# Twenty-four transfers of a convolution cycle, issued in six portions of four, one behind each phase of TensorE

## The chip, the cores and the metric

One core of one Trainium2 chip runs the whole kernel. The metric is the device time of the launch in microseconds (us). Engines are named PE (TensorE matmuls), PEld (its weight loads), DVE (VectorE), ACT (ScalarE), POOL (GpSimd) and SP (SyncE, which here only issues transfers). DMA is the transfer engines, sixteen of them for the core.

## The reference

The input is x, float32, 4 images of 16 channels and 512 x 512 pixels. Four layers follow one another. Layer 0 is a depthwise convolution, window attention and an MLP; layer 1 takes ten steps of a surface flow. Layers 2 and 3, of which the change touches the code, are a residual block each:

```python
def _L2_conv_ref(x, w1, b1, w2, b2):
    out = _conv2d_same(x, w1, b1)      # 3x3, 16 -> 16 channels, float32
    out = jax.nn.relu(out)
    out = _conv2d_same(out, w2, b2)
    return out + x
```

What enters layer 2 is 0.7 u + 0.3 x, where u is the result of the flow and x is the output of layer 0.

## The kernel before, in words

Three stages run one after another: attention_stage, surface_stage and conv_chain. The third, conv_chain, reads two scratch tensors in the chip's main memory, `flowed` (u) and `attended` (x of layer 1), and runs all four convolutions of layers 2 and 3 in one pass over the image, from top to bottom. What follows is about conv_chain alone.

The image's 512 rows are cut into 64 groups of 8 rows. Four groups are held of each input, in `us` and `xs`; `r` is the group's place among them, its number modulo 4. The partitions are 4 images by 32 (16 channels of even rows and 16 of odd rows).

Every engine runs the same sequence of cycles, t = -1 to 66 (`every_cycle`): a few written out, then a loop whose body holds four cycles (`Fori(4, LAST - 7, 4)`, so that it jumps back to its start 13 times), then a few written out again. In cycle t PE makes six phases, in this order:

- conv2 of group t, first half (96 matmuls; it signals c2_begun)
- conv3 of group t - 2 (192 matmuls; c3_made)
- conv2 of group t, second half (96; c2_made)
- conv4 of group t - 2, first half (96; c4_begun)
- conv1 of group t + 1 (192; c1_made)
- conv4 of group t - 2, second half (96; c4_made)

Each matmul is 32 x 32 weights over 512 columns, with a weight load of its own. conv1 and conv3 are written by `across` (L1292), conv2 and conv4 by `along` (L1306). ACT applies bias and ReLU behind conv1 and conv3 (`hide`, `deepen`). DVE mixes the inputs of group t + 2 (`mix`: a scaling of `xs`, then the sum into `image`), adds the residuals behind conv2 (`add_image`) and behind conv4 (`add_middle`, which fills `outs`, one of two buffers, and signals out_done).

SP issues 24 transfers a cycle of 128 KB each: 16 loads of group t + 4, in four quarters of four (quarters 0 and 1 from `flowed` into `us`, quarters 2 and 3 from `attended` into `xs`), and 8 stores of group t - 3. They are placed by `behind(made, m)`, a wait of SP until PE has signalled that phase of group m. Nothing else sets their order: SP's instructions run in the order in which they are written. At the edges of the image `behind` does nothing for a group that is not there. DVE's `mix` waits for all 16 loads of its group, `add_middle` for the stores from the buffer that it fills.

Of the kernel before, what the change touches and what calls it, by code (L numbers as in the profile page):

```python
# [1146 lines left out]
def conv_chain(nc, src, mix_with, dst, weights, bias, edge):  # L1147
# [3 lines left out]
    B, C, HP, W = src.shape  # L1151
# [3 lines left out]
    LAST = GROUPS  # L1155
# [3 lines left out]
    with ExitStack() as ctx:  # L1159
# [3 lines left out]
        def sem(n):  # L1163
            return ctx.enter_context(nc.semaphore("chain_" + n))
# [16 lines left out]
        taps_begun, paced = sem("taps_begun"), sem("paced")  # L1181
        c1_made, c2_begun, c2_made = sem("c1_made"), sem("c2_begun"), sem("c2_made")
        c3_made, c4_begun, c4_made = sem("c3_made"), sem("c4_begun"), sem("c4_made")
        hidden_done, middle_done, deep_done, out_done = (
            sem(n) for n in ("hidden_done", "middle_done", "deep_done", "out_done"))
        stored = [sem(f"stored{k}") for k in range(2)]

        def wait(eng, s, value):

            if not isinstance(value, int) or value > 0:  # L1190
                eng.wait_ge(s, value)

        def there(m):

            return not isinstance(m, int) or 0 <= m <= LAST
# [7 lines left out]
        def every_cycle(eng, cycle):  # L1203

            for t in range(-1, 4):
                cycle(t, t % 4)
            with eng.Fori(4, LAST - 7, 4) as t:
                for k in range(4):
                    cycle(t + k, k)
            for t in range(LAST - 4, LAST + 3):  # L1210
                cycle(t, t % 4)

        def outs_of(m):

            return range(1, G4) if first(m) else range(1) if final(m) else range(G4)
# [3 lines left out]
        @block.sync  # L1219
        def _(sp):  # L1220
            sp.dma_start(w_sb[:], weights).then_inc(w_in, 16)  # L1221
            sp.dma_start(b_sb[:, :], bias).then_inc(w_in, 16)  # L1222
            sp.dma_start(e_sb[:, :], edge).then_inc(w_in, 16)  # L1223

            def load(t, r, quarter):
                if isinstance(t, int) and not 0 <= t < GROUPS:
                    return
                if quarter == 0:
                    wait(sp, mix_done, t - 3)
                    sp.sem_inc(paced, 1)  # L1230
                to, of = ((us, src), (xs, mix_with))[quarter // 2]
                for b in range(B // 2 * (quarter % 2), B // 2 * (quarter % 2 + 1)):
                    for s in range(2):
                        rows = of[b, :, bass.ds(t * (2 * G4) + (PAD + s), 2 * G4 - 1), :]
                        sp.dma_start(to[Q * b + C * s:Q * b + C * s + C, r], rows[:, 0:2 * G4 - 1:2, :]).then_inc(loaded[r], 16)  # L1235

            def store(m, r):
                if not there(m):
                    return
                sp.wait_ge(out_done, m + 1)  # L1240
                sp.sem_inc(paced, 1)
                n, k = len(outs_of(m)), outs_of(m)[0]
                for b in range(B):
                    for s in range(2):
                        rows = dst[b, :, bass.ds(m * (2 * G4) + (2 * k - 2 + s), 2 * n - 1), :]
                        sp.dma_start(rows[:, 0:2 * n - 1:2, :],
                                     outs[Q * b + C * s:Q * b + C * s + C, r % 2, k:k + n]).then_inc(stored[r % 2], 16)

            def behind(made, m):

                if there(m):
                    sp.wait_ge(made, m + 1)
                    sp.sem_inc(paced, 1)

            def cycle(t, r):
                behind(c2_begun, t)
                load(t + 4, r, 0)
                behind(c3_made, t - 2)
                store(t - 3, (r - 3) % 4)
                behind(c2_made, t)  # L1260
                load(t + 4, r, 1)
                behind(c4_begun, t - 2)
                load(t + 4, r, 2)
                behind(c1_made, t + 1)
                load(t + 4, r, 3)

            for t in range(3):
                for quarter in range(4):
                    load(t, t, quarter)
                if t == 0:  # L1270
                    sp.wait_ge(loaded[0], 2 * LOADS)
            every_cycle(sp, cycle)
            store(LAST, LAST % 4)
            for k in range(2):
                sp.wait_ge(stored[k], LOADS * ((LAST - k) // 2 + 1))

# [237 lines left out]
```

## Time and profile before

| what | value |
| --- | --- |
| median of 3 runs | 26449.37 us |
| lowest and highest | 26434.21 and 26502.42 us |
| the profiled execution | 26468.22 us |
| its span, first to last instruction | 26466.4 us |
| mean granted TensorE clock | 0.988 |
| PE busy over the span | 25367.9 us, 96% |

The profile describes one execution, whose own time stands in the table; the rest of the times are of executions that were timed alone. "Idle before" an instruction is what its engine stood still; a releaser is what ended that, and "issue" means that the profile shows none. A share of DMA is the busy time of the sixteen engines over the stretch, averaged; the records of packets overlap a little, so that it can stand above 1. Times within a trace count from the span's start.

### The profile page before, as it was taken

The page shows a single profiled execution, that of the slowest core. Times are in us where ns is not written, and L with a number is a line of the kernel's source. Part 1 is how long each engine was busy: PE and PEld are TensorE (multiplying, and loading weights), DVE is VectorE, ACT ScalarE, POOL GpSimd, SP SyncE. Part 2 cuts the span into 40 slices and gives each one's busy share as a digit, 9 for nine tenths or more (in the row PEclk, how much of TensorE's full clock was granted, in tenths as well). Part 3 has the DMA queues.
Part 4 walks back from the last instruction along what each step waited for, and adds up shares of the span by engine and source line. Part 5 has one row for each costly group of instructions (what it writes and reads, how often), then busy time and mean ns, then how long its engine had stood idle before and what let it go on. Part 6 is the DMA issues. An engine that isn't in the chain of part 4 may idle for free. (4 is left out here: it accounts for less than half of the span.)

```text
span 26466.4 us, 783400 instructions
## 1 busy us (share of the span) xinstructions
PE 25367.9 (96%) x323352; PEld 12517.7 (47%) x323352; DVE 22786.0 (86%) x22077; ACT 22113.8 (84%) x19199; POOL 5851.4 (22%) x6804
## 2 busy tenths in 40 slices
PE   8999999899999999999999999999999999999799
PEld 5666666544444443443444444444534453444455
DVE  6666666699999999999999999999999999999222
ACT  6666666699989998999999899999999998999111
POOL 0000000023323332333233233323323332333000
PEclk9999999999999999999999999999999999999999
DMA  1111111188888888888888888888888888888665
GB/s 33 32 32 32 32 32 32 36 155 156 155 168 156 154 156 169 156 155 166 159 156 155 168 154 156 158 167 156 155 166 158 156 154 168 155 156 157 119 115 101
DMA packets 1550406, 3439.19 MB, mean 130 GB/s; under 512 B 547440, under 2 KB 679152, under 8 KB 1546480
## 3 DMA queue, kind: packets, MB, share of 16 engines
q0 software_dynamic: 805120, 2858.13, 59.7%
q1 hardware_dynamic: 742512, 536.63, 10.3%
q8 instruction: 2649, 43.40, 0.7%
q14 instruction: 125, 1.02, 0.0%
HBM read 294.21 MB, written 201.33 MB: 19 GB/s over the span
## 5 line engine op out<-in xcount | busy, mean ns | idle before, releaser
L910 PE MATMUL surf_ps<-surf_u,surf_matf 64*64 64x512 f32 x87040 | 18836.0, 591 | 386.4 <-SPq L882 161.5
L910 PEld LDWEIGHTS surf_ps<-surf_u,surf_matf 64*64 64x64 f32 x87040 | 7340.4, 133 | 10952.2 <-issue 10767.0
L915 PE MATMUL surf_ps<-surf_deriv,surf_matf 64*64 64x512 f32 x54400 | 12051.1, 593 | 0.0
L915 PE MATMUL surf_ps<-surf_rest,surf_matf 64*64 64x512 f32 x32640 | 7234.5, 589 | 2.9 <-DVE surf_deriv L1078 1.9
L986 ACT ACTIVATE surf_rest<-surf_deriv 128x3072 f32<-128x3072 f32 x1360 | 3766.8, 2770 | 458.4 <-DVE surf_deriv L1089 371.2
L969 ACT ACTIVATE surf_deriv<-surf_ps 128x2048 f32<-128x2048 f32 (+1 forms) x2718 | 3903.7, 1436 | 288.6 <-PE surf_ps L915 282.2
L915 PEld LDWEIGHTS surf_ps<-surf_deriv,surf_matf 64*64 64x64 f32 x54400 | 3728.6, 133 | 29.4 <-issue 23.2
L1043 POOL DMA_DIRECT2D surf_u<-surf_ds x2720 | 2275.1, 973 | 4823.7 <-DVE surf_ds L1137 4334.3
L1115 DVE SCALAR_TENSOR_TENSOR surf_rest<-surf_rest,surf_deriv 128x2048 f32<-128x2048 f32 x1360 | 3106.8, 2284 | 0.3
L1119 DVE SCALAR_TENSOR_TENSOR surf_rest<-surf_deriv 128x2048 f32<-128x2048 f32 x1360 | 3106.6, 2284 | 0.0
L1032 POOL DMA_DIRECT2D surf_rest<-surf_rest x1360 | 1165.3, 857 | 7188.5 <-DVE surf_rest L1115 7170.7
L1071 DVE TENSOR_SCALAR surf_deriv<-surf_deriv 128x1024 f32<-128x1024 f32 (+1 forms) x2722 | 2598.3, 955 | 162.2 <-ACT surf_deriv L969 146.3
L1026 POOL DMA_DIRECT2D surf_rest<-surf_rest x1360 | 1221.1, 898 | 5033.2 <-DVE surf_rest L1082 5032.7
L915 PEld LDWEIGHTS surf_ps<-surf_rest,surf_matf 64*64 64x64 f32 x32640 | 2285.3, 133 | 29.2 <-issue 25.3
L1082 DVE TENSOR_SCALAR surf_rest<-surf_rest,surf_clips 128x1024 f32<-128x1024 f32 x2720 | 2209.8, 812 | 99.4
L1131 DVE SCALAR_TENSOR_TENSOR surf_rest<-surf_ps,surf_dt_ab,surf_rest 128x1024 f32<-128x1024 f32 x1360 | 1737.0, 1277 | 34.4 <-PE surf_ps L915 34.1
L1107 DVE SCALAR_TENSOR_TENSOR surf_rest<-surf_rest,surf_dt_ab 128x1024 f32<-128x1024 f32 x1360 | 1736.1, 1277 | 0.0
L404 ACT ACTIVATE att_hid<-att_w,att_b_fc 128x2048 f32<-128x2048 f32 x256 | 503.8, 1968 | 1466.8 <-PE att_w L275 1466.8
L1076 DVE TENSOR_SCALAR surf_deriv<-surf_ps 128x1024 f32<-128x1024 f32 x1359 | 1655.2, 1218 | 0.0
L1099 DVE SCALAR_TENSOR_TENSOR surf_deriv<-surf_deriv 128x1024 f32<-128x1024 f32 x1360 | 1654.8, 1217 | 0.0
L483 DVE TENSOR_REDUCE att_mx<-att_w 128x32 f32<-128x2048 f32 x512 | 1173.4, 2292 | 522.4 <-PE att_w L204 522.4
L469 DVE SCALAR_TENSOR_TENSOR att_acc<-att_xin,att_vec,att_acc 128x512 f32<-128x512 f32 x2048 | 1535.4, 750 | 54.3
(105 smaller groups left out, 31978.7 us busy)
## 6 DMA issues: line engine op xcount, KB each, us to landing
surf_rest<-surf_rest POOLq DMA_DIRECT2D x4080, 512.0 KB, 5.9
surf_u<-surf_ds POOLq DMA_DIRECT2D x2720, 258.0 KB, 5.0
att_xin<-in_x SPq DMA_DIRECT2D x2048, 41.2 KB, 2.1
attended<-att_out_rows SPq DMA_DIRECT2D x1024, 64.0 KB, 2.1
surf_u<-attended SPq DMA_DIRECT2D x512, 128.0 KB
chain_us<-flowed SPq DMA_DIRECT2D x512, 128.0 KB, 3.8
chain_xs<-attended SPq DMA_DIRECT2D x512, 128.0 KB, 4.7
out<-chain_outs SPq DMA_DIRECT2D x504, 128.0 KB, 2.8
```

The source lines that it names most:

```text
L910: mm = pe.matmul(dst[out, bank(par, phase, CROSS, t), :], matf[rows, mat, :], u[rows, k, t, off + 2:off + 2 + W], start=(i == 0), stop=(i ...
L915: mm = pe.matmul(dst[out, bank(par, phase, DIAG, t), :], matf[rows, mat, :], field(*fields[i], rows=rows, lo=t * W + off, n=W), start=(i = ...
L969: return act.activation(pair(*crossed, *straight, lo, n), made_both(par, phase, lo, n), ACT.Copy)
L986: act.activation(triple("q2", "p2", "B2", par), triple("q", "p", "B", par), ACT.Square).then_inc(squared, 1)
L1043: pool.dma_start(u[rows, k, :, :].rearrange("p a t w -> p (a t w)"), flat(ds[found, :, :]), accum_op=ALU.add).then_inc(u_added, 16)
L1071: return dve.tensor_scalar(both, both, *CLIP)
L1076: return dve.tensor_scalar(pair(*first, *second, 0, W), made_both(par, phase, 0, W), *CLIP)
L1082: return dve.tensor_scalar(f, f, clips[:, which, 0:1], clips[:, which, 1:2], ALU.min, ALU.max)
L1107: dve.scalar_tensor_tensor(out=field("rK", par), in0=field("nK", par), scalar=minus_alpha, in1=field("rK", par), op0=ALU.mult, op1=ALU.mul ...
L1115: dve.scalar_tensor_tensor(out=pair("Ha", par, "Hc", par), in0=pair("q2", par, "p2", par), scalar=1.0, in1=pair("A", par, "C", par), op0=A ...
L1119: dve.scalar_tensor_tensor(out=pair("mB", par, "nK", par), in0=pair("m", 0, "A", par), scalar=-1.0, in1=pair("B", par, "C", par), op0=ALU. ...
L1131: dve.scalar_tensor_tensor(out=field("rH", o), in0=made_side(par, 1, DIAG), scalar=beta, in1=field("rH", o), op0=ALU.mult, op1=ALU.mult).t ...
```

## The change

SP's program is reordered. The eight stores of a cycle are split into two portions of four (images 0 and 1, then 2 and 3), with the wait for out_done ahead of the first alone. A sixth `behind` is added, for c4_made, so that each portion of four transfers has a wait of its own. Half of the stores stays behind c3_made; the other half comes behind c2_made, where quarter 1 of the loads was; the quarters 1, 2 and 3 come behind c4_begun, c1_made and c4_made. No transfer is added, dropped or resized, and no other engine's program is touched.

```diff
--- before.py
+++ after.py
@@ -1234,13 +1234,14 @@
                         rows = of[b, :, bass.ds(t * (2 * G4) + (PAD + s), 2 * G4 - 1), :]
                         sp.dma_start(to[Q * b + C * s:Q * b + C * s + C, r], rows[:, 0:2 * G4 - 1:2, :]).then_inc(loaded[r], 16)
 
-            def store(m, r):
+            def store(m, r, half):
                 if not there(m):
                     return
-                sp.wait_ge(out_done, m + 1)
-                sp.sem_inc(paced, 1)
+                if half == 0:
+                    sp.wait_ge(out_done, m + 1)
+                    sp.sem_inc(paced, 1)
                 n, k = len(outs_of(m)), outs_of(m)[0]
-                for b in range(B):
+                for b in range(B // 2 * half, B // 2 * (half + 1)):
                     for s in range(2):
                         rows = dst[b, :, bass.ds(m * (2 * G4) + (2 * k - 2 + s), 2 * n - 1), :]
                         sp.dma_start(rows[:, 0:2 * n - 1:2, :],
@@ -1256,12 +1257,14 @@
                 behind(c2_begun, t)
                 load(t + 4, r, 0)
                 behind(c3_made, t - 2)
-                store(t - 3, (r - 3) % 4)
+                store(t - 3, (r - 3) % 4, 0)
                 behind(c2_made, t)
+                store(t - 3, (r - 3) % 4, 1)
+                behind(c4_begun, t - 2)
                 load(t + 4, r, 1)
-                behind(c4_begun, t - 2)
+                behind(c1_made, t + 1)
                 load(t + 4, r, 2)
-                behind(c1_made, t + 1)
+                behind(c4_made, t - 2)
                 load(t + 4, r, 3)
 
             for t in range(3):
@@ -1270,7 +1273,8 @@
                 if t == 0:
                     sp.wait_ge(loaded[0], 2 * LOADS)
             every_cycle(sp, cycle)
-            store(LAST, LAST % 4)
+            for half in range(2):
+                store(LAST, LAST % 4, half)
             for k in range(2):
                 sp.wait_ge(stored[k], LOADS * ((LAST - k) // 2 + 1))
```

## Rows read from the trace of the kernel before

**Rows 1.** The page's first line.

```profile
span 26466.4 us, 783400 instructions
```

**Rows 2.** Windows by stage; columns: stretch, length, each engine's busy us, PEclk, DMA share, GB/s.

```profile
24580.00:26466.00 1886.00, 1719.24 (x49152) 1060.74 (x49152) 522.75 (x273) 256.21 (x130) 0.00 (x0) 0.97 0.63 110
```

**Rows 3.** Waits, 24831 to 26194 us: waiter, releaser, us in total, times, longest.

```profile
ACT chain_deep L1367 <- PE chain_ps L1292: 640.5, 48, 17.3
...
DVE chain_outs L1427 <- PE chain_ps L1306: 526.3, 48, 12.5
...
PEld chain_ps L1306 <- issue: 305.2, 478, 5.0
...
PE chain_ps L1306 <- issue: 87.3, 76, 4.1
```

**Rows 4.** Timeline of PE's weight loads at a loop's jump: start, length, instructions, idle before.

```profile
25508.03 2.34 PEld L1292 LDWEIGHTS chain_ps<-chain_image,chain_w 32*32 32x32 f32 x76
...
25512.01 0.65 PEld L1306 LDWEIGHTS chain_ps<-chain_deep,chain_w 32*32 32x32 f32 x33 [1.65 <-issue]
...
25518.50 0.32 PEld L1306 LDWEIGHTS chain_ps<-chain_hidden,chain_w 32*32 32x32 f32 x32 [3.97 <-issue]
```

**Rows 5.** Queues, 24831 to 26194 us: packets, MB, share of the DMA engines.

```profile
q8 instruction: 312, 5.11, 1.9%
```

**Rows 6.** Windows: twelve rounds of the loop, and two cycles after the last load.

```profile
24831.00:26194.00 1363.00, 1268.61 (x36882) 783.59 (x36882) 391.62 (x204) 189.07 (x97) 0.00 (x0) 0.98 0.65 115
...
26329.60:26378.80 49.20, 49.20 (x1558) 38.88 (x1538) 12.83 (x6) 7.87 (x4) 0.00 (x0) 1.00 0.25 47
```

**Rows 7.** Windows of 48 cycles by phase, the sum of each of seven answers.

```profile
sum 163.39, PE 152.69 PEld 78.12 DVE 0.00 ACT 93.86 POOL 0.00; mean PE 3.18 PEld 1.63 DVE 0.00 ACT 1.96 POOL 0.00
...
sum 149.89, PE 124.21 PEld 64.49 DVE 111.06 ACT 0.00 POOL 0.00; mean PE 3.45 PEld 1.79 DVE 3.08 ACT 0.00 POOL 0.00
...
sum 106.70, PE 66.76 PEld 24.12 DVE 67.21 ACT 0.55 POOL 0.00; mean PE 5.56 PEld 2.01 DVE 5.60 ACT 0.05 POOL 0.00
...
sum 301.52, PE 301.52 PEld 221.89 DVE 99.02 ACT 0.00 POOL 0.00; mean PE 6.28 PEld 4.62 DVE 2.06 ACT 0.00 POOL 0.00
...
sum 164.07, PE 157.42 PEld 90.13 DVE 0.00 ACT 94.49 POOL 0.00; mean PE 3.28 PEld 1.88 DVE 0.00 ACT 1.97 POOL 0.00
...
sum 164.22, PE 164.20 PEld 104.18 DVE 114.33 ACT 0.00 POOL 0.00; mean PE 3.42 PEld 2.17 DVE 2.38 ACT 0.00 POOL 0.00
...
sum 306.99, PE 300.90 PEld 197.86 DVE 0.00 ACT 0.00 POOL 0.00; mean PE 6.27 PEld 4.12 DVE 0.00 ACT 0.00 POOL 0.00
```

**Rows 8.** Windows of the six phases of one cycle.

```profile
25570.33:25573.50 3.17, 3.17 (x113) 2.29 (x103) 0.00 (x0) 1.97 (x1) 0.00 (x0) 1.00 1.10 157
25573.50:25577.86 4.36, 3.44 (x107) 1.80 (x102) 3.35 (x2) 0.00 (x0) 0.00 (x0) 1.00 0.76 115
25577.86:25584.21 6.35, 6.35 (x212) 4.70 (x199) 2.43 (x2) 0.00 (x0) 0.00 (x0) 1.00 0.48 85
25584.21:25587.38 3.17, 3.17 (x112) 2.25 (x102) 0.00 (x0) 1.97 (x1) 0.00 (x0) 1.00 0.30 41
25587.38:25590.82 3.44, 3.44 (x120) 2.39 (x102) 2.35 (x1) 0.00 (x0) 0.00 (x0) 1.00 0.90 186
25590.82:25596.50 5.68, 5.68 (x191) 4.12 (x193) 0.00 (x0) 0.00 (x0) 0.00 (x0) 1.00 0.99 173
```

**Rows 9.** Timeline of SP in the same cycle.

```profile
25579.19 1.85 SPq L1235 DMA_DIRECT2D chain_us<-flowed  x4
...
25585.52 5.65 SPq L1246 DMA_DIRECT2D out<-chain_outs  x8
...
25591.42 1.88 SPq L1235 DMA_DIRECT2D chain_us<-flowed  x4
...
25593.48 5.87 SPq L1235 DMA_DIRECT2D chain_xs<-attended  x8
```

**Rows 10.** Windows: the conv2 half that opens a loop body.

```profile
25514.46:25523.56 9.10, 6.01 (x118) 2.33 (x105) 5.78 (x3) 0.05 (x1) 0.00 (x0) 0.68 0.23 48
```

## The prediction

> **What bounds the kernel now.** I read the page first: the span is 26466.4 us [rows 1]. The windows by stage come next, because the edit touches only the last stage: the chain of convolutions holds 1886.0 us of it [rows 2], 7.1% of the whole. 0.3% of the kernel, about what a measurement can tell from no change, is 79 us, so the edit must be worth 4.2% of its stage to be seen.
>
> Then the waits in a stretch of twelve rounds of the loop, 1363 us. Nothing on PE waits for DVE or ACT. ACT waits 640.5 us for PE, in 48 cycles; PE and its weight loads stand only behind "issue", which names no engine and no semaphore: 305.2 us of the weight loads, 87.3 us of the matmuls [rows 3]. So PE sets the pace, and its own lost time has no releaser that the program knows.
>
> What is it? The timeline of the weight loads shows it: a run of 76 breaks off, 1.65 us pass, the next starts in another phase; later 3.97 us pass ahead of conv2's first half [rows 4]. The queue view has the partner: 312 packets of 5.11 MB on an instruction queue, 16 KB each [rows 5]. In the same stretch PE executed 36882 weight loads and 36882 matmuls [rows 6], 236 instructions for each packet. PE's code streams in through DMA packets while it runs, and PE stands still when one is late. The 3.97 us lie where PE's loop jumps back to its first line, conv2(t, 0).
>
> How much is there to win? In the first row of [rows 6] 48 cycles take 1363.0 us, 28.4 each. The second holds two cycles near the end, after the last load (the code is the same, unrolled): 49.2 us, 24.6 each, DMA share 0.25 in place of 0.65. Late code under DMA traffic, the loop's jump included, therefore costs 3.8 us a cycle.
>
> **Where in the cycle.** I cut 48 cycles (24723.1 to 26079.9) at PE's first weight load of each phase and summed each phase. The seven sums of [rows 7] are in this order: conv4 second half (48), conv2 first half without the one that opens a loop body (36), conv2 first half that opens a body (12), conv3 (48), conv2 second half (48), conv4 first half (48), conv1 (48). Means: 3.40, 4.16, 8.89, 6.28, 3.42, 3.42, 6.40 us. A quiet cycle of 24.6 us is eight units of 96 matmuls, 3.075 each, and 6.15 for conv1 and conv3. The excess in an ordinary cycle is then: conv4 second half 0.33, conv2 first half 1.09, conv3 0.13, conv2 second half 0.34, conv4 first half 0.35, conv1 0.25; together 2.49 us.
>
> The phases of one cycle show the traffic behind it [rows 8], in the order conv4 second half, conv2 first, conv3, conv2 second, conv4 first, conv1: DMA share 1.10, 0.76, 0.48, 0.30, 0.90, 0.99. SP's rows give the cause: four loads at 25579.19, 1.3 us behind conv3's start at 25577.86; eight stores at 25585.52, taking 5.65 us to issue, so they run on through conv4's first half; four loads at 25591.42 and eight at 25593.48 over 5.87 us [rows 9]. From the middle of conv2's second half to the end of conv4's, 20 transfers go out; in conv2's first half none. The cost shows one phase behind the traffic, as it must if a packet asked for in one phase is needed in the next:
> - eight stores: 0.35, in conv4's first half
> - twelve loads, DMA full for 3.44 + 5.68 + 3.17 = 12.3 us: 0.25 + 0.33 + 1.09 + 0.13 = 1.80
> - the four loads alone in conv3: 0.34, in conv2's second half.
>
> **The change.** It adds and removes no transfer: still 24 of 128 KB a cycle. Counting from conv3, the portions of four were: 1 in conv3, 2 in conv2's second half, then 3 from the end of conv4's first half to conv4's second half, none in conv2's first. They become one in each: load 0, half the stores, the other half, load 1, load 2, load 3.
>
> *The stores' second half* moves from straight behind the first to behind c2_made, 3.17 us later. out_done was signalled long before, and DVE wants this buffer back two cycles later. The price of eight stores stays 0.35.
>
> *Load 1* moves from behind c2_made to behind c4_begun, into conv1. It is then alone there as load 0 is in conv3, a phase of equal length: 0.34.
>
> *Loads 2 and 3* move to behind c1_made and c4_made: eight loads under 3.17 + 3.17 us. All DMA time of the cycle in [rows 8], share times length, is 3.49 + 3.31 + 3.05 + 0.95 + 3.10 + 5.62 = 19.5 us, 3.25 for one portion: these two phases are full, 6.4 us of it. At the dense price, 1.80 / 12.3 = 0.146 a us, that is 0.94; they are followed at once by load 0, so I take 1.0. Load 0 keeps 0.34.
>
> Sum: 0.35 + 0.34 + 1.0 + 0.34 = 2.03 against 2.49, **-0.46 us a cycle**. There are 58 cycles with full traffic (t = 2 to 59): -27 us. Bounds: if every portion of loads costs what the lone one does, 4 x 0.34 + 0.35 = 1.71, -0.78 a cycle, -45 us. At the other end the queue stays full through three phases; that is the slower rival.
>
> *The jump.* 13 times PE jumps back; the opening conv2 half takes 8.89 us on average, 9.1 in the example, with a granted clock of 0.68 there, that is, that is, between its two levels of 2.4 and 1.2 GHz, after PE stood still for 3.97 us [rows 10]. Today no load is issued in it and its DMA share is 0.23; afterwards load 3 begins 1.3 us behind c4_made, inside the stall. But load 2, under way at the jump, is 4 transfers in place of up to 8. Bound: one late packet more or less, 1.09 us either way. I take +0.5, because two packets must come there and the second meets load 3: +7 us.
>
> *SP itself* gets one more wait and one more count a cycle, in front of load 3. Behind it stand load 3 and the next cycle's load 0. What load 3 brings in cycle t is mixed in cycle t + 2, over 20 us on. Its cover: ACT and DVE wait for PE, never for a transfer, in [rows 3]. Without it the lateness of the last portion, one short phase of 3.2 us, would fall on PE each cycle. *Start:* in cycle -1 two portions of group 3 wait for conv1(0) where one did; 8 transfers at some 0.8 us each leave a crowded start or return later: 0, at most 5 us either way. *End:* the last eight stores go out as before.
>
> -27 + 7 = **-20 us**. The profiled execution took 26468.2 us, 1.8 beyond its span and 19 above the median of 26449.4; it would come to 26448. From the median: **26429 us**.
>
> **A rule beside the trace.** The trace above has PE stopping for late code with DMA busy, and not stopping when it is quiet [rows 4, 6]. The Trainium skill, "Runtime: NRT & Kernel Launch", Instruction fetch mechanics, holds that PE keeps 2048 instructions and that fetches are hidden because the sequencer issues slower than the refill; by that nothing is late and the edit is worth 0, 26449 us, the time of rival 1. The stalls in the trace speak against it. The same section warns that a taken branch forces a fetch before execution goes on, and the 3.97 us agree.
>
> **Rivals.**
> 1. *Depth does not matter, only full engines do.* The DMA work is the same 19.5 us, full or not; the stalls move from conv2's first half to others and the sum stays. For it: 0.90 and 0.99 share cost only 0.35 and 0.25 while the stores drain. Against: the 1.09 behind the densest stretch. Time: 26449, or 26456 with the jump. Chance 0.27. The Trainium skill, "DMA: Bandwidth & Descriptors", Queues, rings and completion order, says that a DMA engine goes round its queue rows packet by packet, so that a code packet would wait for one packet of SP's at most, however many stand behind; by it the time would be the 26449 of this rival. No row here shows a single engine's order.
> 2. *Faster by over 0.3%: smooth traffic makes no code late.* The cycle goes down toward 24.6: 58 x 2.49 = -144 us, 26305; half of that is -72, so it decides once more than 55% of the excess goes. For it: one of the lone four loads costs 0.34 / 4 = 0.085 us, one of the dense twelve 1.80 / 12 = 0.15. Against: conv2's first half loses its pause. Chance 0.12.
> 3. *Slower by over 0.3%: the pause was what let the queue drain.* Load 2, load 3 and load 0 follow each other with no gap, the backlog stands from conv1's end through conv3, and a packet is late by today's worst, 1.09 us, in each of conv2's first half, conv3 and conv2's second half; with 0.34 and 0.35 for the rest that is 3.96 a cycle, +1.47, +85 us, and +14 at the jumps: 26548. It decides from +1.25 a cycle on. For it: conv4's second half and conv2's first need 6.5 us of DMA in 6.3 us. Against: conv3 has 6.3 us for its 3.25. Chance 0.07.
>
> **The numbers.** My case has 0.54 and runs from 26398 (-45, and -6 at the jumps) to 26463 (0, and +14 at the jumps). The scatter of the runs shown (26434 to 26502) is as large as the effect. The range, 26380 to 26495, takes in rival 1 whole, the lone-portion bound, the scatter, and part of rival 2. Faster 0.12, same 0.81, slower 0.07.
>
> **What would show it.** Right: SP's rows in groups of four with a gap between each; conv2's first half below 4.16 or equal, conv4's second half near 3.4, conv3 or conv2's second half a few tenths up; DMA share in conv2's first half near 1.0 and in conv1 near 0.5; the twelve rounds some 1340 us; "issue" of the weight loads still over 300 us a stretch. Wrong: an ACT or DVE wait for a transfer, PE's "issue" halved (rival 2), conv3 above 7 us (rival 3), or opening conv2 halves far from 9 us.

## The result, and the profile after

The changed kernel takes 26536.96 us (median of 13 runs, 26515.65 to 26562.36) against 26464.21 us of the kernel before (13 runs, 26429.56 to 26502.42). The ratio is 1.0028, 95% interval 1.002 to 1.0036: about 73 us slower. That is just inside the 0.3% which I had taken as no change, but clear of the noise, and outside the range.

The first line of the changed kernel's page:

```profile
span 26527.2 us, 783465 instructions
```

The windows of the twelve rounds of the loop, counted at PE's first weight load from the first loop body to the thirteenth (48 cycles), first in the kernel before, then in the changed one. The second row of the changed kernel is two cycles after the last load:

```profile
24723.30:26084.44 1361.14, 1268.49 (x36879) 780.77 (x36864) 395.06 (x206) 188.94 (x96) 0.00 (x0) 0.98 0.65 115
```

```profile
24726.09:26138.55 1412.46, 1288.08 (x36879) 759.36 (x36864) 396.27 (x207) 188.90 (x96) 0.00 (x0) 0.98 0.63 111
...
26390.30:26439.10 48.80, 48.80 (x1550) 38.06 (x1537) 12.83 (x6) 7.87 (x4) 0.00 (x0) 1.00 0.24 47
```

51.3 of the 60.8 us between the two spans lie in these 48 cycles, and the chain has ten more with loads. The quiet cycles are as fast as in [rows 6], 24.4 us. So the loss is in the cycles with loads.

The waits of the changed kernel in twelve rounds:

```profile
ACT chain_deep L1371 <- PE chain_ps L1296: 659.2, 48, 19.9
...
DVE chain_outs L1431 <- PE chain_ps L1310: 523.6, 48, 12.3
...
PEld chain_ps L1310 <- issue: 332.2, 498, 5.8
PE chain_ps L1310 <- issue: 104.7, 84, 4.9
PEld chain_ps L1296 <- issue: 100.5, 245, 2.3
PE chain_ps L1296 <- issue: 19.7, 32, 1.4
```

The last two rows stood at these values in the kernel before, in the twelve rounds of [rows 3]:

```profile
PEld chain_ps L1292 <- issue: 57.2, 183, 1.3
PE chain_ps L1292 <- issue: 5.5, 12, 0.9
```

Against [rows 3] no new releaser has come: PE still waits for no engine, ACT and DVE still for PE. "Issue" has grown everywhere, 305.2 to 332.2 and 87.3 to 104.7 us in conv2 and conv4, and most of all in the weight loads of conv1 and conv3, 57.2 to 100.5 us. No transfer's data came too late.

Is a late packet of code really what ends these stops? The packets of the two traces say so. In the 48 cycles of the kernel before, the starts of two weight loads in a row lie more than 0.6 us apart 182 times, 264 us in all; 129 of the 181 distances from one such stop to the next lie within 1.5 weight loads of a multiple of 127.5. That is 255 matmuls and weight loads, where [rows 5] and [rows 6] have one packet of 16 KB for 236 of them, the jumps included. Half of the stops end between 1.42 and 1.71 us behind the landing of a 16 KB code packet. After the change there are 219 stops, 326 us.

The phases, as in [rows 7] and in the same order (conv4 second half, conv2 first half in ordinary cycles, the one that opens a loop body, conv3, conv2 second half, conv4 first half, conv1):

```profile
sum 163.93, PE 154.03 PEld 81.91 DVE 0.00 ACT 94.06 POOL 0.00; mean PE 3.21 PEld 1.71 DVE 0.00 ACT 1.96 POOL 0.00
...
sum 129.36, PE 124.65 PEld 71.38 DVE 91.30 ACT 0.00 POOL 0.00; mean PE 3.46 PEld 1.98 DVE 2.54 ACT 0.00 POOL 0.00
...
sum 124.10, PE 72.73 PEld 22.11 DVE 66.41 ACT 0.40 POOL 0.00; mean PE 6.06 PEld 1.84 DVE 5.53 ACT 0.03 POOL 0.00
...
sum 325.73, PE 307.36 PEld 194.21 DVE 119.54 ACT 0.00 POOL 0.00; mean PE 6.40 PEld 4.05 DVE 2.49 ACT 0.00 POOL 0.00
...
sum 194.33, PE 162.54 PEld 81.46 DVE 0.00 ACT 94.45 POOL 0.00; mean PE 3.39 PEld 1.70 DVE 0.00 ACT 1.97 POOL 0.00
...
sum 164.86, PE 164.50 PEld 102.53 DVE 114.32 ACT 0.00 POOL 0.00; mean PE 3.43 PEld 2.14 DVE 2.38 ACT 0.00 POOL 0.00
...
sum 304.50, PE 301.48 PEld 205.75 DVE 0.00 ACT 0.00 POOL 0.00; mean PE 6.28 PEld 4.29 DVE 0.00 ACT 0.00 POOL 0.00
```

| phase | before, us | after, us | difference over 48 cycles |
| --- | --- | --- | --- |
| conv4 second half | 3.40 | 3.42 | +0.5 |
| conv2 first half, ordinary (36) | 4.16 | 3.59 | -20.5 |
| conv2 first half, opening a body (12) | 8.89 | 10.34 | +17.4 |
| conv3 | 6.28 | 6.79 | +24.2 |
| conv2 second half | 3.42 | 4.05 | +30.3 |
| conv4 first half | 3.42 | 3.43 | +0.6 |
| conv1 | 6.40 | 6.34 | -2.5 |

The gain in conv2's first half is there, -20.5 us; conv3 and conv2's second half take 54.5 back, and the jump 17.4 more.

One of the twelve opening halves is that of the first loop body, which PE enters from above, without a jump. It is short, here before and after:

```profile
24723.10:24727.94 4.84, 3.81 (x108) 1.85 (x104) 3.67 (x3) 0.00 (x0) 0.00 (x0) 1.00 0.09 13
```

```profile
24725.89:24729.90 4.01, 3.81 (x108) 1.85 (x104) 2.88 (x2) 0.00 (x0) 0.00 (x0) 1.00 0.79 132
```

The eleven halves behind a jump therefore take (106.70 - 4.84) / 11 = 9.26 us before and (124.10 - 4.01) / 11 = 10.92 after.

The windows of one cycle's six phases, in the order of [rows 8]:

```profile
25571.73:25575.49 3.76, 3.65 (x114) 1.81 (x97) 0.00 (x0) 1.97 (x1) 0.00 (x0) 1.00 0.48 96
25575.49:25579.02 3.53, 3.53 (x115) 2.05 (x103) 2.42 (x2) 0.00 (x0) 0.00 (x0) 1.00 0.84 129
25579.02:25585.54 6.52, 6.52 (x202) 3.79 (x193) 3.35 (x2) 0.00 (x0) 0.00 (x0) 1.00 0.96 124
25585.54:25590.34 4.80, 3.49 (x108) 1.49 (x103) 0.00 (x0) 1.97 (x1) 0.00 (x0) 1.00 0.51 99
25590.34:25593.78 3.44, 3.44 (x108) 1.84 (x98) 2.35 (x1) 0.00 (x0) 0.00 (x0) 1.00 0.45 86
25593.78:25600.03 6.25, 6.25 (x208) 4.44 (x192) 0.00 (x0) 0.00 (x0) 0.00 (x0) 1.00 0.75 135
```

The timeline of SP in that cycle, and that of PE's weight loads (rows with the long stops):

```profile
25572.77 5.58 SPq L1235 DMA_DIRECT2D chain_xs<-attended  x8
25579.99 1.87 SPq L1235 DMA_DIRECT2D chain_us<-flowed  x4
25586.85 6.71 SPq L1247 DMA_DIRECT2D out<-chain_outs  x8
25594.89 1.86 SPq L1235 DMA_DIRECT2D chain_us<-flowed  x4
```

```profile
25582.12 0.25 PEld L1296 LDWEIGHTS chain_ps<-chain_middle,chain_w 32*32 32x32 f32 x31 [0.79 <-issue]
...
25587.94 0.24 PEld L1310 LDWEIGHTS chain_ps<-chain_hidden,chain_w 32*32 32x32 f32 x32 [2.22 <-issue]
```

Conv4's second half has fallen from a DMA share of 1.10 to 0.48, as meant. But conv3 has risen from 0.48 to 0.96: loads 2 and 3 begin at 25572.77, load 0 at 25579.99, and the twelve keep the DMA engines busy from the middle of conv4's second half to the end of conv3. PE then stands 0.79 us inside conv3 and 2.22 us inside conv2's second half, where [rows 8] have a conv2 second half of 3.17 us.

### The profile page after: what moved, and what is told of

Read it like the earlier page. It is cut to its first block and busy times, and to the rows that moved or that the text cites. A ratio compares the mean times of both kernels' runs of the same rounds, so it can differ in the third digit from the quotient of the medians.

```text
span 26527.2 us, 783465 instructions
## 1 busy us (share of the span) xinstructions
PE 25398.3 (96%) x323352; PEld 12579.4 (47%) x323352; DVE 22782.7 (86%) x22077; ACT 22109.3 (83%) x19199; POOL 5839.0 (22%) x6804
```

## The experiments

All kernels keep PE's, ACT's and DVE's programs as they are unless said, so only SP's order differs. "48 cycles" is the window shown above; it is one profiled execution of each kernel, so a few tens of us between two of them say little unless the ratios agree. A diff is against the changed kernel where nothing else is said. Ratios are to the kernel before, run on the same chip, with the 95% interval.

**One part at a time.** The stores split, the loads where they were (against the kernel before; the call above it stores the first half):

```diff
                 behind(c2_made, t)
+                store(t - 3, (r - 3) % 4, 1)
                 load(t + 4, r, 1)
```

> The kernel before with one part of the change: the eight stores split into two fours (behind c3_made and behind c2_made), load 1 right behind the second four, loads 2 and 3 where they were. The changed kernel takes 12 of its ratio's thousandths... in numbers: 26537 against 26464 us, ratio 1.0028, and its 48 cycles cut by phase take 1412.5 us against 1361.1. Theory P (the pause): the cost is that loads 2, 3 and 0 now follow each other through conv2's first half, where nothing was issued before; splitting the stores costs nothing: ratio 0.9995 to 1.0005, 48 cycles 1355 to 1370 us. Theory S (the stores): four stores that now reach into conv4's first half and make load 1 later are the cost: ratio 1.002 or more, 48 cycles over 1390 us. Theory D (only the sum of DMA work counts, places shift code packets by luck): anything, with no order between this run and the others.

(Its opening has a slip; the figure meant is the ratio 1.0028.) Measured: 0.9993 (0.9984 to 1.0002), 48 cycles:

```profile
24702.43:26052.10 1349.67, 1259.98 (x36879) 805.83 (x36865) 395.76 (x207) 188.90 (x96) 0.00 (x0) 0.98 0.67 116
```

Splitting the stores costs nothing; theory S falls.

The loads moved, the stores whole:

```diff
                 store(t - 3, (r - 3) % 4, 0)
-                behind(c2_made, t)
                 store(t - 3, (r - 3) % 4, 1)
                 behind(c4_begun, t - 2)
```

> The other part alone: the eight stores together behind c3_made as before, loads 1, 2 and 3 behind c4_begun, c1_made and c4_made as in the changed kernel. Theory P: the whole cost is here: ratio 1.002 to 1.0035, 48 cycles 1400 to 1420 us, conv3 near 6.8 and conv2's second half near 4.0 us. Theory S: as before, ratio under 1.0008, 48 cycles under 1370 us.

Measured: 1.003 (1.0019 to 1.0041), 48 cycles:

```profile
24731.69:26161.96 1430.27, 1297.00 (x36879) 748.48 (x36864) 395.05 (x206) 188.96 (x96) 0.00 (x0) 0.98 0.63 110
```

The whole cost is in the loads' places.

**The pause, meant to be given back.** The changed kernel without the wait for c4_made:

```diff
                 load(t + 4, r, 2)
-                behind(c4_made, t - 2)
                 load(t + 4, r, 3)
```

> The changed kernel with one line taken out, the wait for c4_made in front of load 3: loads 2 and 3 go out together behind c1_made, and conv2's first half issues nothing again. Theory P: the cost is gone: ratio 0.998 to 1.0005, 48 cycles 1335 to 1370 us, conv3 back under 6.4 us, the conv2 half that opens a loop body back near 8.9. Theory S: the cost stays: ratio 1.002 and more, 48 cycles over 1395 us.

Measured: 1.0031 (1.0019 to 1.0044). The windows of its 48 cycles, and the sum of its 48 conv3:

```profile
24736.46:26164.75 1428.29, 1293.02 (x36879) 784.46 (x36865) 394.80 (x206) 188.96 (x96) 0.00 (x0) 0.97 0.64 110
...
sum 340.49, PE 313.83 PEld 196.55 DVE 117.94 ACT 0.00 POOL 0.00; mean PE 6.54 PEld 4.09 DVE 2.46 ACT 0.00 POOL 0.00
```

The forecast fails: conv3 is even longer, 340.49 / 48 = 7.09 us. But the edit did not give the pause back, and so it does not test theory P. SP's issues in one cycle, and the first weight loads of the conv2 half that follows:

```profile
25593.47 4.95 SPq L1235 DMA_DIRECT2D chain_xs<-attended  x8
```

```profile
25596.29 1.26 PEld L1309 LDWEIGHTS chain_ps<-chain_hidden,chain_w 32*32 32x32 f32 x41
```

Eight transfers released at c1_made take SP until 25598.42, 2.1 us into conv2's first half. Counted over the ordinary cycles of each trace, SP issues 0.1 loads in that half in the kernel before, 4.2 in the changed one and still 3.6 here. What P needs, a conv2 first half without loads, was not made.

The wait taken out only in front of the jump:

```diff
-                behind(c4_made, t - 2)
+                if r != 3:
+                    behind(c4_made, t - 2)
```

> The changed kernel with that wait taken out only in the last cycle of each loop body (r = 3), so that at PE's jump back no load is newly issued, and the other three cycles of four stay as changed. If the stall at the jump grows because load 3 is issued inside it (it went from 8.89 to 10.34 us in the conv2 half that opens a body, 17 us in 12 of them): that half goes back to 8.9 us and conv3 behind it stays at 6.35; 48 cycles near 1393 us, ratio 1.0018 to 1.0023. If the loads of the jump are not what lengthens it: 10.3 us and 1412 us stay.

Measured: 1.0034 (1.0021 to 1.0048). The windows of its 48 cycles, and the sum of the 12 conv2 halves that open a body:

```profile
24714.42:26145.42 1431.00, 1297.49 (x36879) 768.77 (x36864) 395.35 (x207) 188.93 (x96) 0.00 (x0) 0.97 0.63 110
...
sum 125.96, PE 72.96 PEld 22.46 DVE 66.43 ACT 0.30 POOL 0.00; mean PE 6.08 PEld 1.87 DVE 5.54 ACT 0.02 POOL 0.00
```

The mean of the twelve is 10.50 us, 11.09 behind the jumps (10.92 in the changed kernel). This does not test the idea either: without the wait SP still issues 4.9 loads in the opening half (5.2 in the changed kernel). At one jump:

```profile
25545.30 5.19 SPq L1235 DMA_DIRECT2D chain_xs<-attended  x8
```

```profile
25551.53 0.32 PEld L1311 LDWEIGHTS chain_ps<-chain_hidden,chain_w 32*32 32x32 f32 x32 [4.36 <-issue]
```

The eight go out until 25550.49, and the stall runs from 25547.17 to 25551.53. Whether the loads issued inside it or those already under way lengthen it stays open.

**Is it the loads' bytes?** Both orders with each load cut to a quarter of its columns; the transfers' number and all waits stay. The rest of the two buffers is zeroed once ahead of the first load (two memsets of DVE and a wait of SP, not shown), so the convolutions work on other data than the reference's:

```diff
-  sp.dma_start(to[Q * b + C * s:Q * b + C * s + C, r], rows[:, 0:2 * G4 - 1:2, :])
+  sp.dma_start(to[Q * b + C * s:Q * b + C * s + C, r, :, 0:W // 4], rows[:, 0:2 * G4 - 1:2, 0:W // 4])
```

> The kernel before with every load cut to a quarter of its columns (128 of 512); the rest of the two input buffers is zeroed once and then read as it is, so the convolutions work on other data. Number and place of the transfers and all waits stay. If the traffic of the loads is what makes code late: ordinary cycles fall from 27.2 to 25.0 us or less and the opening conv2 half from 8.9 to under 8; 48 cycles near 1230 us, ratio near 0.995. If the traffic has nothing to do with it: 48 cycles stay at 1361 us.

> The changed kernel with the same cut of the loads to a quarter of their columns. If the difference between the two orders (51 us in 48 cycles) comes from the bytes of the loads under way, it goes to under 15 us here; if it comes from when SP issues (its waits, its own instructions), it stays near 50 us.

Measured: 0.9936 (0.9921 to 0.9951) in the order before, 0.9939 (0.9924 to 0.9954) in the changed order. The 48 cycles, before's order and then the changed one:

```profile
24716.39:25964.10 1247.71, 1207.59 (x36884) 895.72 (x36864) 394.69 (x206) 188.93 (x96) 0.00 (x0) 0.98 0.31 65
```

```profile
24698.34:25943.94 1245.60, 1206.32 (x36884) 896.39 (x36865) 394.71 (x206) 188.91 (x96) 0.00 (x0) 0.99 0.31 65
```

This is the clearest pair. With light loads the two orders are equal, 1247.7 and 1245.6 us where they were 51 apart, and 113 us of the 48 cycles of the order before are gone. SP's waits and the number of its transfers are the same; only the bytes have changed. So the cost of the change is the loads' traffic making PE's code late, and nothing in SP's own waits. The stops agree: 45 over 0.6 us in place of 182, none of them at such a distance from the last.

One part of the forecast missed: the opening half was to fall under 8 us. A cycle without a jump, two halves behind a jump, and the sum of the twelve opening halves, in the order before with light loads:

```profile
24845.85:24870.41 24.56, 24.56 (x784) 18.50 (x773) 8.13 (x4) 3.94 (x2) 0.00 (x0) 1.00 0.32 68
```

```profile
24919.52:24928.06 8.54, 5.55 (x111) 2.12 (x96) 5.78 (x3) 0.00 (x0) 0.00 (x0) 0.80 0.07 17
25023.17:25031.85 8.68, 4.49 (x111) 1.51 (x97) 5.78 (x3) 0.00 (x0) 0.00 (x0) 1.00 0.07 19
...
sum 101.04, PE 64.08 PEld 23.42 DVE 66.03 ACT 0.00 POOL 0.00; mean PE 5.34 PEld 1.95 DVE 5.50 ACT 0.00 POOL 0.00
```

The cycles without a jump run like the quiet ones of [rows 6], 24.56 us against 24.6. The halves behind a jump hardly gain: 8.86 us (the first of the twelve, 3.53 us, is entered without one; this cut is within 0.1 us of the one above) where the kernel before has 9.26, at a DMA share of 0.07. So most of the price of a jump is there with hardly any traffic. Nor is it the clock: the half at a granted clock of 1.00, 8.68 us, is no shorter than the one at 0.80.

**Other places for the loads.** All loads in the two long phases, two portions at a time:

```diff
                 load(t + 4, r, 0)
+                load(t + 4, r, 1)
...
                 behind(c4_begun, t - 2)
-                load(t + 4, r, 1)
-                behind(c1_made, t + 1)
                 load(t + 4, r, 2)
-                behind(c4_made, t - 2)
                 load(t + 4, r, 3)
```

> The changed kernel with its loads in pairs of portions, in the two long phases alone: loads 0 and 1 behind c2_begun (conv3), stores in two fours as in the change, loads 2 and 3 behind c4_begun (conv1); nothing is issued behind c1_made or c4_made. Theory L (lateness: what costs is how much of the loads is issued behind c1_made, because it is still under way in conv2's first half, at the jump and ahead of load 0): ordinary cycles cost less than in the changed kernel (28.2 us), the conv2 half that opens a body goes back to 8.9 to 9.4 us, ratio 0.998 to 1.0005. Theory R (room: eight loads need a long phase, wherever it lies): the same gain in conv1, and the eight loads in conv3 cost no more than the eight in conv1 did, conv2's second half under 3.8 us; ratio 0.997 to 0.999. If loads near conv3 are dear for another reason: conv3 and conv2's second half together over 11 us, ratio over 1.002.

Measured: 1.002 (1.001 to 1.003), 48 cycles and the sum of its 48 conv1:

```profile
24738.96:26159.97 1421.01, 1279.64 (x36879) 768.13 (x36865) 394.61 (x206) 188.96 (x96) 0.00 (x0) 0.99 0.66 110
...
sum 339.88, PE 321.70 PEld 187.44 DVE 0.00 ACT 0.00 POOL 0.00; mean PE 6.70 PEld 3.90 DVE 0.00 ACT 0.00 POOL 0.00
```

Both theories miss: the late end is gone, each eight has a long phase, and it is slow all the same. conv1, where eight start at once, takes 7.08 us in place of 6.40.

Everything as early as it can be:

```diff
                 store(t - 3, (r - 3) % 4, 1)
+                load(t + 4, r, 1)
                 behind(c4_begun, t - 2)
-                load(t + 4, r, 1)
-                behind(c1_made, t + 1)
                 load(t + 4, r, 2)
-                behind(c4_made, t - 2)
                 load(t + 4, r, 3)
```

> Loads earlier than in any kernel so far: load 0 behind c2_begun and the stores in two fours as in the change, then load 1 right behind the second four of stores (c2_made) and loads 2 and 3 behind c4_begun; nothing behind c1_made or c4_made. Beside the run with the split stores alone (ratio 0.9993, 48 cycles 1349.7 us, conv2's opening half 9.3 us) only load 3 is moved, from c1_made forward to c4_begun. Theory L (lateness): another step the right way: opening half 9.0 us or less, ordinary cycles at or under 26.8 us, 48 cycles 1325 to 1345 us, ratio 0.997 to 0.9993. Theory D (depth of the queue): the twelve loads are denser, so conv1 and conv4's second half rise by more than conv2's first half falls: 48 cycles over 1355 us, ratio over 1.000.

Measured: 1.0025 (1.0015 to 1.0036). Its 48 cycles, the sum of the 36 ordinary first halves of conv2, and one of them in the timeline of the weight loads:

```profile
24705.13:26120.11 1414.98, 1271.40 (x36879) 809.66 (x36864) 396.14 (x207) 188.94 (x96) 0.00 (x0) 0.97 0.65 111
...
sum 197.38, PE 127.64 PEld 62.59 DVE 155.44 ACT 0.00 POOL 0.00; mean PE 3.55 PEld 1.74 DVE 4.32 ACT 0.00 POOL 0.00
...
25573.18 0.24 PEld L1308 LDWEIGHTS chain_ps<-chain_hidden,chain_w 32*32 32x32 f32 x32 [2.76 <-issue]
```

Theory L falls and D is right about the total, but not about the place: nothing is issued in conv2's first half, and yet it is 197.38 / 36 = 5.48 us, 2.76 of it one stop in the example. Against the split kernel only the wait of load 3 lies one phase earlier, and the 48 cycles got 65 us longer (the ratios, 0.9993 and 1.0025, agree). In time the step is small: loads 2 and 3 are issued in 4.87 us here (x8 from 25562.78, done 1.5 us before conv2's first half begins at 25569.17) and in 7.87 us in a cycle of the split kernel (x8 from 25595.73).

How full the queue is shows on the code packets. I took the stops that end 1.1 to 1.9 us behind the landing of a code packet and looked at the next code packet. With no transfer of SP under way when PE resumes, it starts a median of 1.14 us later in this run and 1.17 in the kernel before; with one to four under way 1.15 and 1.27; with more than four 3.21 and 2.41. The packet itself takes 1.08 and 0.96 us with none under way, 1.54 and 1.52 with more than four. So a deep queue goes with a code packet that starts late, more than with one that moves slowly. The depth of the queue counts.

**One portion late at a time,** each diff against the split kernel (1349.67 us). Load 3 alone, from c1_made to c4_made:

```diff
-                behind(c1_made, t + 1)
+                behind(c4_made, t - 2)
                 load(t + 4, r, 3)
```

> The kernel with the split stores alone (ratio 0.9993, 48 cycles 1349.7 us) and one load portion moved: load 3 from c1_made to c4_made, as in the change; loads 1 and 2 stay at c2_made and c4_begun. Cut by phase the split kernel has 4.20 in conv2's first half, 6.30 in conv3, 3.37 in conv2's second half (ordinary cycles). Theory Q (a code packet in conv2's first half and in conv3 that meets load 3 and then load 0): the cost of the change comes with load 3 alone: conv3 plus conv2's second half rise by 1 us or more, the opening half by 1 us, conv4's second half and conv2's first fall by under 1 us together; 48 cycles 1385 to 1415 us, ratio 1.001 to 1.003. Theory N (all three loads together, the DMA engines full through conv4's second half and conv2's first): with load 3 alone there is a pause before it, so at most a third of the cost: 48 cycles under 1370 us, ratio under 1.0005.

Measured: 1.0013 (1.0004 to 1.0023). Its 48 cycles, and the sums of conv3 and of conv2's second half:

```profile
24726.21:26117.71 1391.50, 1287.52 (x36879) 764.29 (x36864) 394.75 (x206) 188.88 (x96) 0.00 (x0) 0.98 0.64 113
...
sum 321.79, PE 308.38 PEld 196.94 DVE 118.24 ACT 0.00 POOL 0.00; mean PE 6.42 PEld 4.10 DVE 2.46 ACT 0.00 POOL 0.00
...
sum 184.39, PE 162.78 PEld 79.66 DVE 0.00 ACT 94.45 POOL 0.00; mean PE 3.39 PEld 1.66 DVE 0.00 ACT 1.97 POOL 0.00
```

Load 1 alone, from c2_made to c4_begun:

```diff
-                load(t + 4, r, 1)
                 behind(c4_begun, t - 2)
+                load(t + 4, r, 1)
                 load(t + 4, r, 2)
```

> The split kernel with one other portion moved: load 1 from c2_made to c4_begun, where load 2 follows it at once; load 3 stays at c1_made, nothing is issued in conv2's first half. Theory Q: this alone costs nothing or little in conv3 and at the jump: 48 cycles 1345 to 1370 us, ratio 0.999 to 1.0005. Theory N: it makes the twelve loads end one phase later, which shows in conv2's first half (over 4.8 us in ordinary cycles) and at the jump (over 10 us): 48 cycles over 1390 us, ratio over 1.0015.

Measured: 1.0004 (0.9995 to 1.0013). Its 48 cycles, and the sum of the 36 ordinary first halves of conv2:

```profile
24742.36:26128.93 1386.57, 1269.83 (x36879) 798.76 (x36865) 395.52 (x207) 188.96 (x96) 0.00 (x0) 0.98 0.67 113
...
sum 167.00, PE 124.84 PEld 61.67 DVE 128.14 ACT 0.00 POOL 0.00; mean PE 3.47 PEld 1.71 DVE 3.56 ACT 0.00 POOL 0.00
```

Load 3 is the larger part: 53 us by the ratios (0.9993 to 1.0013), 42 by the 48 cycles, and it shows in conv3 (6.70 us) and conv2's second half (3.84), the phases of the change's own loss; theory Q holds for it. For load 1 nothing is shown. The ratios differ by 29 us, but their intervals overlap; the 48 cycles differ by 37, in single executions. And SP's issues barely moved: in the split kernel the stores keep SP until about c4_begun, so load 1 goes out in conv1 in either kernel; in ordinary cycles both issue 7.7 loads there.

**The jump.** Eight cycles in a loop body, so that PE jumps 6 times in place of 13, with the split stores and with the changed order:

```diff
-            with eng.Fori(4, LAST - 7, 4) as t:
-                for k in range(4):
-                    cycle(t + k, k)
+            with eng.Fori(4, LAST - 11, 8) as t:
+                for k in range(8):
+                    cycle(t + k, k % 4)
```

> The split kernel with eight cycles in a loop body in place of four: PE jumps back 6 times in place of 13. If each jump costs what the phase means say, 9.34 - 4.20 = 5.1 us, 7 of them give 36 us: ratio 0.9975 to 0.9985. If an opening half is long for another reason (its place among the transfers), nothing: 0.9993. It would be the fastest order found here.

> The changed kernel with eight cycles in a loop body. With its order a jump costs 10.37 - 3.59 = 6.8 us by the phase means: 7 fewer give 47 us, ratio 1.0028 - 0.0018 = 1.0008 to 1.0013. If the jump's extra of the change (1.45 us each) is only moved to another phase: 36 us, ratio 1.0014 to 1.0017.

Measured: 0.9981 (0.9972 to 0.999) with the split stores, 26430.56 against 26480.04 us, and 1.0014 (1.0005 to 1.0023) with the changed order. Against 0.9993 and 1.0028 that is 32 and 37 us for seven jumps, 4.5 and 5.3 us each. Both are rough, since in each pair the two intervals overlap, and the jumps are not all that changes: in the changed order conv3 takes 7.9 to 10.0 us on average in the last four cycles of the long body and 6.3 to 7.5 in its first four, perhaps because the code packets fall at other places there. The first kernel is faster than both kernels of the study.

## Why the prediction was wrong

**What held.** The bound: PE, with its code arriving late under DMA traffic. The pair with light loads shows it. The stores' split cost nothing. Conv2's first half became shorter (3.59 us), conv4's second half stayed (3.42), the phase behind load 1 alone in conv1, conv4's second half, has an excess of 0.34 as I had it; but it had 0.33 under the twelve dense loads too, so that this is no proof of the price. No transfer's data came late, SP's added wait cost nothing that a row shows, and all that lies outside the 48 cycles (ten cycles with loads, start and end) grew by 9.5 us.

**The step that failed** is the price of loads 2 and 3 with load 0 behind them: 1.0 for the two and 0.34 for load 0, together 1.34. Measured as excess over a quiet cycle's phases they are 0.51 in conv2's first half, 0.64 in conv3 and 0.97 in conv2's second half: 2.12 us. I had written that load 0 "keeps 0.34". It could not: 0.34 was the price of four loads on an empty queue, with conv3 at a share of 0.48, and after the change conv3 runs at 0.96. The run with load 3 alone moved late shows the same: conv3 6.70 and conv2's second half 3.84 us. My own dense price, 0.15 for each of twelve, would have given 1.80 and with it no gain at all. The rest of the sum is 0.34 + 0.36 + 0.19 = 0.89 against 0.69. In all 3.01 us in place of 2.03: +0.52 a cycle where I forecast -0.46, +30 us over 58 cycles.

**The second term** is the jump. I took +0.5 us, with bounds of 1.09 either way; it is +1.66 (9.26 to 10.92 us), outside them. 13 of them are +22 us. My 8.89 for the half today was a mean that took in the one without a jump. Of the +1.66, 0.54 is longer busy time of PE (5.72 to 6.27 us); the granted clock read 0.67 to 1.00 in these halves before and 0.69 to 0.85 after, and no run separates the clock's share. The two terms give +52, where the profiled spans differ by 60.8 and the medians by 73; single runs scatter over 73 us before and 47 after.

**The 3.8 us a cycle** that I laid to late code under DMA traffic, the jump included, is two things. The light loads take 113.4 us off 48 cycles, 2.4 a cycle: that is traffic. Of the rest nearly all is the jump, and with light loads it was still there.

**Rival 3** comes nearest to the mechanism: the pause let the queue drain, and without it packets are late in conv2's first half, in conv3 and in conv2's second half. For it stands that the orders which issue about four loads in conv2's first half (the change, the loads moved alone, the pause meant to be given back, load 3 later) are those with a long conv3 and a long second half of conv2. The three phases are the right ones but for their sizes (0.51, 0.64, 0.97 in place of 1.09 each); so the loss was 73 us in place of 99, and under the 79 from which I let it decide. I gave it 0.07 because conv3 "has 6.3 us for its 3.25". The argument counted room on average; the next code packet starts later the more transfers are under way at that moment. Rival 1, depth without effect and an unchanged sum, is refuted by the result itself, 73 us for the same transfers, and by the early loads.

**What the other orders add.** Two moves from the split kernel have a price that the ratios show: load 3 one wait earlier +85 us (+65 in 48 cycles) and load 3 one wait later +53 (+42). The later one runs on into load 0, as in the change. The earlier one makes the twelve loads denser, as do the loads in the long phases. It is not the number of transfers behind one wait that decides: the split kernel releases four stores and load 1 together and costs nothing, and in the kernel before SP issues loads 1, 2 and 3 in one go all the same [rows 9], because its stores hold it up. Why that density is cheap and a slightly greater one dear was not taken apart.

The Trainium skill, "DMA: Bandwidth & Descriptors", Queues, rings and completion order, has each DMA engine go round its queue rows packet by packet. Alone it would make the depth of SP's queue irrelevant; the early loads, with a conv2 first half 1.3 us longer than before, and the later start of a code packet behind more than four transfers speak against that as a full account.

**Open.** Why twelve dense loads cost 1.80 us in the old place and 2.12 in the new one is not settled. The jump lies in the new place, and so does DVE's mixing of group t + 2, which reads the same buffers; neither was taken apart. No run kept conv2's first half free of loads with the rest of the change in place, so the pause itself is untested. Nor does any run show where a late code packet stands in its DMA engine.

## What to carry to other kernels

An engine's code can stream in through the same DMA engines as the data; then data transfers that nobody waits for still set its pace: look for "issue" gaps at regular distances and for the instruction queue's packets. A price read off a batch on an empty queue holds only there; before moving a batch, look at what is still under way where it lands and at what follows it. A wait moved in the program need not move a transfer: look at when the engine issues. An even spread over the phases is no aim in itself: no other placing of the loads that was tried beat that of the kernel before, and the fastest kernel came from a longer loop body.

## What the hardware showed that I had not expected

- Loads under way cost PE 113 us in 48 cycles (1361.1 against 1247.7 us) although no engine waited for their data: what they delayed was PE's own code.
- A jump back in PE's loop costs about 5 us (9.26 against 4.16 us for the half behind it), and it costs nearly as much with little traffic: 8.86 us with light loads, at a DMA share of 0.07. With the changed order it is 10.92. The Trainium skill, "Runtime: NRT & Kernel Launch", Instruction fetch mechanics, warns of a stall at a taken branch; these halves agree and give it a size.
- Moving the wait of four transfers of 128 KB one phase forward, with nothing else changed, made the kernel 85 us longer by the ratios (0.9993 to 1.0025) and its 48 cycles 65 (1349.7 to 1415.0).
- With more than four transfers of SP under way the next code packet started 2.41 and 3.21 us after PE resumed, with none 1.17 and 1.14 (medians of the kernel before and of the early loads).
